# Attention on one core: two rows of key blocks in each call of the values' product, and other f32 products moved beside these calls

## What is computed

```python
xn = layer_norm(x, in_ln_w, in_ln_b)
proj = xn @ W_in.T + b_in
q, k, v, p, y = jnp.split(proj, [D_EXP, 2 * D_EXP, 3 * D_EXP, 4 * D_EXP], axis=-1)
```

## Time and profile before

| What | before |
|---|---|
| median of three runs | 1658.05 us (1657.13 to 1660.45) |
| the profiled execution, its own time | 1660.07 us |
| its span in the profile | 1658.3 us |
| PE, matmuls | 1385.7 us, 84% of the span |
| DVE | 1140.3 us, 69% |
| ACT | 706.1 us, 43% |
| POOL | 436.3 us, 26% |
| granted PE clock over the span | 0.979 |

### The profile page before, as it was taken

How to read it: one execution, slowest core, us unless ns; L and a number is a source line. 1 busy time by engine, 2 the same in 40 slices (tenths; PEclk the granted TensorE clock), 3 DMA queues, 4 the chain that set the end, 5 groups by cost and what they waited for, 6 DMA issues and landing times. The chain is left out here.

```text
span 1658.3 us, 65686 instructions
## 1 busy us (share of the span) xinstructions
PE 1385.7 (84%) x27370; PEld 1024.7 (62%) x27370; DVE 1140.3 (69%) x5594; ACT 706.1 (43%) x2475; POOL 436.3 (26%) x818
## 2 busy tenths in 40 slices
PE   5788888888888888888888886479999999999886
PEld 4667777777777777777777775335555555555443
DVE  5767777777777777777777776456576766676485
ACT  3333223222222222222222222126777777777765
POOL 2001111111111111111111112435245535522354
PEclk9999999999999999999999999968999999999898
DMA  5200000000000000000000000158537735751001
GB/s 119 28 4 5 5 6 5 5 7 5 5 7 5 5 7 5 5 7 5 5 6 5 5 7 5 39 108 136 69 69 107 98 58 85 118 64 20 1 14 38
DMA packets 68941, 53.70 MB, mean 32 GB/s; under 512 B 12686, under 2 KB 68390, under 8 KB 68646
## 3 DMA queue, kind: packets, MB, share of 16 engines
q1 hardware_dynamic: 66470, 49.32, 18.2%
q10 hardware_dynamic: 2176, 0.20, 0.1%
HBM read 31.84 MB, written 15.47 MB: 29 GB/s over the span
## 5 line engine op out<-in xcount | busy, mean ns | idle before, releaser
L731 PE MATMUL PS<-GB,W 128*128 128x8 f16 x18432 | 575.5, 168 | 178.6 <-DVE GB L1041 174.4
L731 PEld LDWEIGHTS PS<-GB,W 128*128 128x128 f16 x18432 | 532.4, 104 | 287.2 <-DVE GB L1041 282.4
L2289 DVE TENSOR_REDUCE MX<-PS 128x1 f32<-128x512 f32 (+3 forms) x352 | 220.7, 636 | 139.0 <-PE PS L1807 137.2
L935 ACT ACTIVATE tr<-PS 128x16 f32<-128x16 f32 x512 | 94.2, 184 | 490.9 <-PE PS L731 490.7
L2057 ACT ACTIVATE PT<-PS 128x512 f32<-128x512 f32 (+1 forms) x352 | 193.1, 565 | 120.9 <-PE PS L1823 115.2
L937 ACT ACTIVATE tz<-PS 128x16 f32<-128x16 f32 x512 | 94.2, 184 | 192.5 <-PE PS L731 192.5
L1027 DVE SCALAR_TENSOR_TENSOR u_<-tr,PS 128x16 f32<-128x16 f32 x512 | 87.8, 172 | 124.8 <-PE PS L731 112.9
L685 POOL TENSOR_TENSOR rt<-mv,eps 128x1 f32<-128x1 f32 x96 | 18.4, 191 | 554.0 <-DVE mv L1052 554.0
L1034 DVE SCALAR_TENSOR_TENSOR zg<-tz,HR 128x16 f32<-128x16 f32 x512 | 90.5, 177 | 80.9 <-ACT tz L937 80.8
L1804 PE MATMUL PS<-KS,QS 99*128 99x256 bf16 (+3 forms) x512 | 134.6, 315 | 11.9 <-DVE MX L2289 7.9
L1820 PE MATMUL PS<-QS,KS 102*128 102x256 bf16 (+3 forms) x512 | 130.6, 306 | 3.9 <-ACT PT L2057 2.6
(11 more groups left out here) (393 smaller groups left out, 2505.6 us busy)
## 6 DMA issues: line engine op xcount, KB each, us to landing
QS<-q_parts SPq DMA_DIRECT2D x90, 128.0 KB, 11.1
KS<-k_parts SPq DMA_DIRECT2D x90, 128.0 KB, 13.5
q_parts<-PQ SPq DMA_DIRECT2D x16, 384.0 KB, 11.2
k_parts<-PK SPq DMA_DIRECT2D x16, 384.0 KB, 3.2
X<-XM SPq DMA_DIRECT2D x32, 64.0 KB
out_dram<-X SPq DMA_DIRECT2D x8, 256.0 KB, 2.3
XM<-in_L_attn_x_dram SPq DMA_DIRECT2D x16, 80.0 KB
s_hh<-in_L_attn_w_hh_dram SPq DMA_DIRECT2D x1, 768.0 KB, 5.7
```

Of the source, the lines that this page charges most:

```text
L731: return pe.matmul(bank[:, p, at:at + B], W[:, kc, w:w + P], state[:, part, kc, :], start=False, stop=True, skip_group_check=True)
L935: act.activation(as_states(tr), now(pR), ACT.Tanh, scale=gate_scale).then_inc(hn_tr.sem, 1)
L2289: dve.tensor_reduce(MX[:, g % 2, heads[0]:heads[-1] + 1, NT - 1 - it], p_x[:, k % 2, 0:len(heads) * w].rearrange("p (a w) -> p a w", w=w), ...
```

## The change

The exponentials get a buffer for all four rows (`PT_OF`). `times_v` is then called for rows 0 and 1 together in slot 9, and for rows 2 and 3 together in slot 0 of the next quarter. Other f32 products of PE are moved into the slots of these two calls and of the turned heads (slot 3 of a quarter): the gates and c = 0 from 6 to 9, c = 1 and 2 from 8 and 9 to 11, c = 3 from 10 to 14, the position product as a whole to 14, the values' t = 0 and 1 to 31 and t = 2 and 3 to 36, the turned gated heads from 21 and 24 to 20 and 25, both halves of the output product to 27. The steps of ACT, DVE and POOL that follow them are moved as well. Nothing is computed otherwise, and the number of instructions stays. In the diff the lines from 1568 on are POOL's, those from 1700 PE's, those from 1984 ACT's and those from 2144 DVE's.

```diff
-            PT = sb(ctx, "PT", [P, 2, 4, S])
+            PT = sb(ctx, "PT", [P, 10 * S])
+            PT_OF = [PT[:, 4 * P * at:4 * P * (at + NT - j)].rearrange("p (i w) -> p i w", i=4)
+                     for j, at in enumerate((0, 4, 7, 9))]
...
@@ -1605,7 +1607,7 @@
-                    for c in {8: (0,), 10: (1,), 14: (2,), 16: (3,)}.get(i, ()):
+                    for c in {11: (0,), 13: (1,), 16: (2,), 18: (3,)}.get(i, ()):
...
@@ -1709,7 +1711,7 @@
-                    if i == 6:
+                    if i == 9:
...
-                    for c in {6: (0,), 8: (1,), 9: (2,), 10: (3,)}.get(i, ()):
+                    for c in {9: (0,), 11: (1, 2), 14: (3,)}.get(i, ()):
...
-                    for t in {12: (0, 1), 13: (2,), 14: (3,)}.get(i, ()):
+                    for t in range(NT if i == 14 else 0):
...
@@ -1772,7 +1774,7 @@
-                    for t in {29: (0,), 31: (1,), 33: (2,), 35: (3,)}.get(i, ()):
+                    for t in {31: (0, 1), 36: (2, 3)}.get(i, ()):
...
-                        last = pe.matmul(p_o[32 * i:32 * i + 32, j * P:S], VV[:, p, j, 4 * g + i, :], PT[:, j % 2, i, 0:S - j * P],
+                        last = pe.matmul(p_o[32 * i:32 * i + 32, j * P:S], VV[:, p, j, 4 * g + i, :], PT_OF[j][:, i, :],
...
-                    if j >= 1 and n == len(ITEMS[j]) - 1:
-                        if j == 1:
-                            if g == 0:
-                                pe.wait_ge(vv.sem, vv.value(pe, b))
-                            if not (isinstance(b, int) and b == 0 and g == 0):
-                                pe.wait_ge(o_kept.sem, o_kept.value(pe, b, g))
-                        times_v(b, p, g, j - 1)
+                    if j == 2 and n == len(ITEMS[j]) - 1:
+                        if g == 0:
+                            pe.wait_ge(vv.sem, vv.value(pe, b))
+                        if not (isinstance(b, int) and b == 0 and g == 0):
+                            pe.wait_ge(o_kept.sem, o_kept.value(pe, b, g))
+                        times_v(b, p, g, 0)
+                        times_v(b, p, g, 1)
 
                 def values_late(b, p, g, k):
                     if k == 0:
-                        times_v(b, p, g, NT - 1).then_inc(o_ps.sem, 1)
+                        times_v(b, p, g, 2)
+                        times_v(b, p, g, 3).then_inc(o_ps.sem, 1)
...
@@ -1883,7 +1886,7 @@
-                    for c in {21: (1,), 24: (0,)}.get(i, ()):
+                    for c in {20: (1,), 25: (0,)}.get(i, ()):
...
-                    for half in {26: (0,), 27: (1,)}.get(i, ()):
+                    for half in range(2 if i == 27 else 0):
...
@@ -1992,7 +1994,7 @@
-                    for c in {7: (0,), 9: (1,), 10: (2,), 11: (3,)}.get(i, ()):
+                    for c in {10: (0,), 12: (1,), 13: (2,), 15: (3,)}.get(i, ()):
...
-                    if i == 8:
+                    if i == 12:
...
-                    for t in {30: (0,), 32: (1,), 34: (2,), 36: (3,)}.get(i, ()):
+                    for t in {32: (0,), 33: (1,), 37: (2,), 38: (3,)}.get(i, ()):
...
-                    for c in {22: (1,), 25: (0,)}.get(i, ()):
+                    for c in {22: (1,), 26: (0,)}.get(i, ()):
...
@@ -2194,14 +2196,14 @@
-                    if i == 7:
+                    if i == 10:
...
-                    if i == 9:
+                    if i == 13:
...
-                    for c in {12: (0,), 14: (1,)}.get(i, ()):
+                    for c in {14: (0,), 16: (1,)}.get(i, ()):
...
-                    for t in {31: (0,), 33: (1,), 35: (2,), 37: (3,)}.get(i, ()):
+                    for t in {33: (0,), 34: (1,), 38: (2,), 39: (3,)}.get(i, ()):
```

More of the change, by code:

```diff
@@ L1335, in build @@
             p_b = PS[:, 7, :]
-            bvr = PT[:, 0, 0:2, :]
-            bvp = PT[:, 1, 0:2, :].rearrange("p a n -> p (a n)").bitcast(BF16)[:, 0:6 * DE].rearrange("p (k n) -> p k n", k=3)
+            bvr = PT[:, 0:2 * S].rearrange("p (a n) -> p a n", a=2)
+            bvp = PT[:, 4 * S:6 * S].bitcast(BF16)[:, 0:6 * DE].rearrange("p (k n) -> p k n", k=3)
             bv = signal("v_bias_parts")
@@ L1969, in _ @@
                     if i == 1:
-                        output(*last, 21)
-                        output(*last, 24)
+                        output(*last, 20)
+                        output(*last, 25)
                     if i >= 1:
@@ L1976, in _ @@
                     if i == 1:
-                        output(*last, 26)
                         output(*last, 27)
@@ L2056, in item @@
                     act.wait_ge(e_ps.sem, e_ps.value(act, b, k + 1))
-                    act.activation(PT[:, j % 2, heads[0]:heads[-1] + 1, 0:w],
+                    act.activation(PT_OF[j][:, heads[0]:heads[-1] + 1, :],
                                    p_e[:, k % 2, 0:len(heads) * w].rearrange("p (a w) -> p a w", w=w),
@@ L2129, in _ @@
                         output(*last, 22)
-                        output(*last, 25)
+                        output(*last, 26)
                     if i >= 2:
@@ L2243, in split @@
                     def split(c):
-                        rest = PT[:, 0, 3, :]
+                        rest = PT[:, 3 * S:4 * S]
                         dve.wait_ge(kk2.sem, c + 1)
```

## The result

The changed kernel takes **1712.72 us** (median of four runs, 1711.96 to 1714.48) against 1658.11 for the kernel before beside it, four runs too: 1.0324 times, with a 95% interval of [1.0311, 1.0336]. It is slower, as forecast, but by 54.6 us and not by 33: 0.7 us above the upper end of the range, 1712. The lines named here are numbered two higher than before, those of PE's turned heads three; the two kernels with added matmuls have two more on each.

What follows compares the result with a forecast made beforehand. PE sets the pace but stands where ACT's chain is uncovered. Quarters of -0.3+3.2+0.9+1.6 make 5.4 us a sequence, 33 in all on the profiled 1660.07, so 1693, or 1691 for the median; range 1664 to 1712.

Steps and rivals of the forecast that it cites:

- cover taken from ACT's chain: Slots 10 to 7: f32 work moved away had covered ACT's chain, so PE stands; 5.4 us more in a sequence.
- The walk per quarter: Each quarter followed from slot 10's exponential: quarter 0 0.3 us less, quarters 1 to 3 3.2, 0.9 and 1.6 more.
- The wait for KF_ before the position product: Quarter 1: the position product starts at 8.03, PE's own work would allow 6.6, so PE stands 1.4 us.
- c = 2 waits 0.32 for QF: Quarter 1: PE ready for c = 2 at 2.21 us after slot 10's exponential starts, QF done at 2.63, start 2.68.
- the two rivals that I kept outside the forecast: Attention: falling clock, 15 us on top, chance 0.14; smear behind POOL's gated product, 1696 us, chance inside the forecast's 0.65.
- the clock: Quarter 1, six sequences: clock falls after standing and 16-column products, 2.5 us each, 15 in all, 1706; chance 0.14.
- the smear behind the gated product: Quarter 1, five sequences: DVE's smear waits for POOL's product, M of slot 8 1 us later, 1696; inside the 0.65.
- point A: Start of slot 10's exponential on ACT; E of slot 2 cannot start earlier than 2.60 us after it.
- the lock: Quarter 1: DVE's two-SBUF-input smear is blocked while POOL's operation holds the shared ports; M of slot 8 1 us later.
- my upper bound: Joined calls: one entry and exit saved, at most 0.24 us a join, 15.4 in all; 0.19 and 12.2 taken.
- quiet quarter: Sequences 6 and 7, g = 0: joining rows 2 and 3 gains nothing, rows 0 and 1 the whole 0.19 us.
- the waits of slots 2 and 3: Quarter 3: VV and TH precede the exponentials of slots 0 and 1; E of slot 3 starts at 4.2 us.

Runs made afterwards that it cites:

- `gate_fill`: Changed kernel with POOL's gated product in slot 8 instead of 15 and unread 512-column matmuls added to slot 14; 1694.16 us, 1.0192 times the kernel before.
- `gate_early`: Changed kernel with POOL's gated product issued in slot 8 instead of 15; 1696.2 us, 1.0223 times the kernel before.
- `fill_clock`: Changed kernel with seven unread matmuls of 512 columns added to slot 14; 1714.19 us, 1.0324 times the kernel before.
- `join_again`: Kernel before with only the joined calls, all other steps in their old slots, run once more; 1653.49 us, 0.996 times the kernel before.
- `join_only`: Kernel before with only the joined calls, all other steps in their old slots; 1653.26 us, 0.9969 times the kernel before.
- `v_back`: Changed kernel with the values' products and their ACT and DVE steps back in the old slots; 1697.91 us, 1.0223 times the kernel before.

## Why the prediction was right and wrong

**Right.** The sign, and the cause: cover taken from ACT's chain. The walk per quarter stands as follows: quarter 0 13.2 forecast, 13.35 measured; quarter 2 16.4 and 16.25; quarter 3 14.5 and 15.05; quarter 1 19.8 and, with both disturbances taken away, 19.57 (in `gate_fill`, of which some 0.6 are the fillers between the parts) or 19.0 (sequence 1 of `gate_early`). So the walk of quarter 1 was 0.8 too long, which hid some of what follows. The wait for KF_ before the position product, forecast 1.4 from the end of PE's stream, has 0.75 in its row; c = 2 waits 0.32 for QF; sequence 7 stayed as it was, 134.8 and 134.4 us to the end.

**Wrong: the two rivals that I kept outside the forecast both came true, and together.** I gave the clock 0.14 and left the smear behind the gated product at +1 inside my range, though my own walk had POOL start 0.15 us ahead of the smear. Added to the forecast, their prices of 15 and 5 give 1711, a sum that the prediction never made. In quarter 1 of sequence 3 the prediction's point A (the start of slot 10's exponential) lies at 1333.00 + 0.21 = 1333.21. M of slot 8 was forecast at A+14.75 and came at 1349.42, A+16.21: 1.46 late, where the rival's price is 1.0. All of it is the lock: with the clock still at 1.00 `fill_clock` has M of slot 8 at the same place, and from the quarter's first matmul it is 16.42 against the undisturbed 14.30 of `gate_early`, so that the lock costs 2.1. From there to the end of the quarter I had 19.6 - 14.75 = 4.85, and it took 1356.73 - 1349.42 = 7.31: 2.46 more, at a granted clock of 0.50 for most of it. The same stretch took 4.70 in `gate_fill`, at 1.00, so the clock cost 2.6 (the rival said 2.5); the joined call alone took 3.02 in it (1352.09 to 1355.11) instead of 1.64. Lock and clock make 4.7 in this sequence; less the 0.8 that the walk was too long, 3.9 are missing in quarter 1, and 18.6 in five sequences, of the 20 in all.

The failed step is the chance of the clock and the price of the lock, and behind them a fault of reasoning: I treated the two as independent accidents. The smear makes the stand before slot 8, and either stand lets the clock fall. In sequences 1 to 5 together, removing the smear's brought 14.9 us, filling the other one nothing, and both 19.5. Nor do their prices simply add. In sequence 3 of `gate_early`, where the clock fell ahead of the second smear, the quarter lost 3.6 (22.6 against 19.0; 0.7 of it in the smear, which then met another operation of POOL), and M of slot 8 came at 16.09 in place of 14.30. In the changed kernel that early part doesn't count, since PE waits for the smear and the end of POOL's product anyway.

The page "SBUF — State Buffer" of the Trainium skill, section on the two sides of SBUF, makes the lock a matter of which operation starts first. The traces agree. The smear ended 0.55 us after the product that had started 0.02 ahead of it, and in `gate_early` 0.55 after the two-input operation of 1338.64 (1339.79 and 1340.34); in the earlier trace rows it was 0.53. The other way round, in sequence 1 of `gate_early`, the smear started 0.16 ahead of POOL's copy and took 0.75, and the copy took 1.06 where it took 0.61 in sequence 2. What the smear costs is what POOL has just begun.

**Joins.** Two single calls, of 512 and 384 columns, take 1.00 and 0.79 with 0.09 ahead of each, 1.97; the joined one 1.64 and 0.09, 1.73. A join saves 0.24, my upper bound and not the 0.19 that I took: of the 1.64, seven times 0.213 are the stream, and the 0.15 left is what one single call has too, so the seam costs nothing that can be seen. By the rule on weight loads of the page "TensorE: Matmul & The Clock Gate" of the Trainium skill, Part 3, a join would have been worth 0.13; these rows don't agree, and the weight loads at the seam of the joined call in `join_again` start while its matmuls go on:

```profile
1354.22 0.13 PEld L1854 LDWEIGHTS PS<-PT,VV 128*32 128x32 f32 x4 [0.30 <-issue]
```

What I missed is that a join also moves cover. In a quiet quarter, where rows 0 and 1 should have given their whole 0.19, it got shorter by 0.13 only (10.69 to 10.56): in `join_only` M of slot 8 comes 0.79 us after that of slot 7, where the matmuls between take 0.67. Eight joins are worth 1.9 us of PE's time in a sequence and bring 0.3.

**Smaller sizes.** Quarter 3 was 0.5 too short in the walk: I had the waits of slots 2 and 3 (0.90 in its row), but not those of slots 8 and 9 (0.37 and 0.34), which DVE ends. Sequence 0 was forecast at +4.2 and gave 2.7, all of it ahead of its first slot (1121.14 to 1123.81; 1120.45 in `v_back`, so that it goes with the moved values); sequence 6 at +1.7, measured +2.7 (49.99 to 52.65).

## What to carry to other kernels

Before work is merged into fewer, longer calls, ask of each piece that moves which wait of an in-order neighbour it was hiding; here a join saved 0.24 us of PE's time, and the moves made with it cost 7.4 us in a sequence. A stand of PE that a move creates is to be priced together with the clock, and stands close to each other together: here the fall came at whichever was left. A long POOL operation does not belong where DVE's next two-input operation gates PE (here it cost 2.1 us a sequence), and a lead of 0.15 us in a walk is a coin toss, not a margin.

## What was not expected of the hardware

Half the granted clock over the whole GRU, 1019 us of the span, costs nothing that can be seen: its last group of products starts at 1018.11 at a clock of 1.00 and at 1018.23 at 0.50. Whole runs give no steady difference either. At the lower mean clock two runs of the changed kernel are 1.9 us longer than the two others, and five of `join_again` 2.0 longer than the three others, but two of `fill_clock` are 4.4 shorter. In quarter 1 of the attention the same fall, for some 10 us, cost 2.6 us beside the lock, and 3.6 where the gated product was out of the way.

The fall itself is not strict. In `gate_early`, five sequences with the same instructions spent between 0 and 10 us at half clock, and quarter 1 took from 19.0 to 22.6 us.
